# Reordering the hand-over from attention to the expert tiles in a fused two-layer kernel

## What is computed

```python
# layer 0, attention: summaries of 64-token chunks (4 sequences of 512), 16 heads, added to x
# layer 0, feed-forward block, _forward:
h = rmsnorm(x, ln1_w); q, k, v = ...            # 16 query heads, 4 key/value heads of 8
out = softmax(causal(q k^T / sqrt(8))) v         # over all 2048 tokens
out = out * sigmoid(out @ Wg + bg)
x = x + out @ Wo + bo
h2 = rmsnorm(x, ln2_w)
top1 = argmax(h2 @ Wr + br)                      # router, 8 experts
u = h2 @ W1[top1] + b1                           # up product, 128 -> 2 x 256
y = (u1 * sigmoid(u2)) @ W2[top1] + b2           # gate, down product
return x + y
# layer 1: a Mamba-like scan with 4 heads, then a ternary feed-forward part
```

## Time and profile before

| | us |
|---|---|
| median of 3 runs | 603.2 (603.0 to 603.21) |
| the profiled execution | 603.02 |
| its span | 600.9 |
| mean granted TensorE clock | 0.994 of full |
| busy: TensorE / ScalarE / VectorE / GpSimd | 562.0 / 470.0 / 399.1 / 120.8 |

### The profile page before, as it was taken

One profiled execution on the slowest core, in us unless ns is written; L12 is line 12 of the kernel. 1 busy time (PEld: TensorE's weight loads), 2 busy tenths in 40 slices (PEclk: granted clock), 3 DMA queues, 4 the chain that ended last, 5 costly groups with the idle time before them and its releaser, 6 DMA issues.

```text
span 600.9 us, 11244 instructions
## 1 busy us (share of the span) xinstructions
PE 562.0 (94%) x3944; PEld 330.8 (55%) x3944; DVE 399.1 (66%) x1060; ACT 470.0 (78%) x669; POOL 120.8 (20%) x161
## 2 busy tenths in 40 slices
PE   6899999999999999999887899698699999999998
PEld 3343434443443434333334587386478887887887
DVE  6784887666363453685527355887888788698773
ACT  5699999989899999999795366479598686685673
POOL 2063221120020030103601355112012010010010
PEclk9999999999999999999999999999999999999999
DMA  7212011024222210400317220200000000000000
GB/s 223 47 25 67 2 27 47 11 88 159 89 107 107 89 72 2 137 6 14 112 42 227 66 77 37 83 2 0 1 1 2 1 17 1 2 17 1 2 19 17
DMA packets 30982, 30.72 MB, mean 51 GB/s; under 512 B 6848, under 2 KB 20960, under 8 KB 30928
## 3 DMA queue, kind: packets, MB, share of 16 engines
q1 hardware_dynamic: 29680, 27.45, 14.6%
q0 software_dynamic: 1248, 2.57, 1.2%
HBM read 13.44 MB, written 12.89 MB: 44 GB/s over the span
## 4 chain that ended last, share of the span: by engine, by line
PE 70%; DVE 15%; ACT 7%; issue 6%; DMA 1%; POOL 0%; DVEq 0%; ACTq 0%; another core or an unknown queue 0%; POOLq 0%
PE ps L1414 18%; PE ps L1393 9%; PE ps L92 6%; PE ps L94 6%; PE ps L93 5%; ACT r L1002 3%; PE ps L1725 2%; PE ps L1494 2%; PE ps L1600 1%; PE ps L1307 1%; PE ps L1763 1%; PE ps L1766 1%; PE ps L1486 1%; PE ps L1730 1%; PE ps L1267 1%
## 5 line engine op out<-in xcount | busy, mean ns | idle before, releaser
L1002 ACT ACTIVATE r<-ps 128x1024 f32<-128x1024 f32 x272 | 257.5, 1041 | 19.6 <-PE ps L1393 17.0
L1414 PE MATMUL ps<-r 128*32 128x512 f32 (+3 forms) x1280 | 144.8, 539 | 0.9 <-DVE r L2185 0.5
L858 POOL TENSOR_SCALAR_AFFINE_SELECT r<-r 128x512 f32<-128x512 f32 (+1 forms) x80 | 47.0, 589 | 206.0 <-ACT r L1002 205.7
L1393 PE MATMUL ps<-r2r 32*128 32x512 f32 (+3 forms) x640 | 80.2, 445 | 4.2 <-ACT r L1002 2.5
L1393 PEld LDWEIGHTS ps<-r2r 32*128 32x128 f32 x640 | 35.6, 182 | 46.9 <-ACT r L1002 21.3
L901 POOL TENSOR_TENSOR r<-r 128x512 f32<-128x512 f32 x16 | 22.6, 1414 | 151.0 <-ACT r L1210 130.1
L1414 PEld LDWEIGHTS ps<-r 128*32 128x32 f32 x1280 | 27.7, 108 | 40.5 <-issue 27.3
L94 PE MATMUL ps<-r2r 128*128 128x512 f32 (+1 forms) x104 | 39.0, 375 | 0.0
L1279 PE MATMUL ps<-consts 128*128 128x512 bf16 x98 | 25.4, 400 | 8.4 <-DMA consts<-in_consts 4.4
L93 PE MATMUL ps<-r2r 128*128 128x512 f32 (+1 forms) x88 | 32.7, 372 | 0.0
L876 POOL DMA_INDIRECT rows_by_token<-r x23 | 23.6, 1025 | 23.8 <-ACT r L1065 14.1
(11 more groups left out here) (436 smaller groups left out, 1206.6 us busy)
## 6 DMA issues: line engine op xcount, KB each, us to landing
rows_by_expert<-r SPq DMA_DIRECT2D x34, 258.0 KB, 2.5
r2r<-r2r SPq DMA_DIRECT2D x56, 64.0 KB, 2.0
r<-in_f_W SPq DMA_DIRECT2D x1, 2048.0 KB, 9.4
r<-rows_by_expert SPq DMA_DIRECT2D x23, 64.5 KB, 1.8
res<-in_x SPq DMA_DIRECT2D x4, 256.0 KB, 4.0
r<-in_g_h1T SPq DMA_DIRECT2D x1, 1024.0 KB
r<-in_g_h2T SPq DMA_DIRECT2D x1, 1024.0 KB
r<-rows_by_token SPq DMA_DIRECT2D x4, 256.0 KB, 4.0
```

The source lines that it names most:

```text
L858: pool.affine_select(blk, blk, pattern, ALU.is_ge, nothing, base=0, channel_multiplier=-1).then_inc(s_msk, 1)
L1002: act.activation(probs[:, n % PBUFS, :, :], ps[:, b:b + 2, :], ACT.Exp).then_inc(s_exp, 1)
L1393: m = pe.matmul(ps[:, 2 * (n % SBUFS) + h, at:at + TB - query], kst[32 * j:32 * j + 32, group, P * kt:P * kt + P], qst[32 * j:32 * j + 32, ...
L1414: m = pe.matmul(ps[32 * j:32 * j + 32, 6, query:TB], vp[:, kt, group, :], probs[:, (2 * v + j // 2) % PBUFS, j % 2, at:at + TB - query], s ...
```

## The change

- **W1 high parts.** Eight pieces of 512 columns in place of four of 1024 (four after the last attention step, four behind `first_slots_copied`). VectorE's low piece n waits for high piece n. Low piece 6 moves from ahead of the read of LOGITS to the end of the early tiles, beside piece 7.
- **Router products first.** At the LOGITS step TensorE runs one `kept_busy` product in place of `first_up(1)`; `first_up(1)` now stands behind the router products.
- **Late rows.** The four `rows_scaled` instructions of VectorE go. ScalarE does them as Copy with a scale per partition: two after `up_tanh_of(1)`, two after `up_tanh_of(2)`. GpSimd's scatter of tile i waits for its own row tile.
- **Gate of the second early tile.** `activated(1)` stands between `late_expert` and `late_placed`, where VectorE would wait for the ranks, not behind them.
- **Row numbers ahead of experts.** VectorE computes `rows_of_tiles` before it copies `expert_i` and compares `pick`; the copy now has a settle of its own.
- **SyncE** reads two row numbers, not four, before it waits for the scatters.
- **Bias product.** In the loop the wait for the high rows stands behind the bias product, not ahead of it.

```diff
-        W1HIGH = [(w1f[:, a:a + 1024], w1h[:, a:a + 1024]) for a in range(0, 4096, 1024)]
-        W1LOW = [(w1f[:, a:a + 512], w1h[:, a:a + 512], w1l[:, a:a + 512]) for a in range(0, 4096, 512)]
+        W1SPLIT = [(w1f[:, a:a + 512], w1h[:, a:a + 512], w1l[:, a:a + 512]) for a in range(0, 4096, 512)]
@@ sync
-            ahead = [first_row(t) for t in range(AHEAD, AHEAD + 2 * GROUP)]
+            ahead = [first_row(t) for t in range(AHEAD, AHEAD + GROUP)]
             sp.wait_ge(s_scat, 16 * NT)
             for t in range(AHEAD, SLOTS):
-                r = ahead[t - AHEAD] if t < AHEAD + 2 * GROUP else first_row(t)
+                r = ahead[t - AHEAD] if t < AHEAD + GROUP else first_row(t)
@@ gpsimd
-                pool.wait_ge(s_h2, 2 if i < NT - 2 else 3)
+                pool.wait_ge(s_h2, 2 + i - (NT - TPB))
@@ scalar
+            def late_rows_scaled(tiles_of):
+                for i in tiles_of:
+                    act.activation(h2[i], xn[:, i, :], ACT.Copy, scale=hs2[:, i:i + 1]).then_inc(s_h2, 1)
@@
                 if k == STEPS:
-                    up_weights_high(0)
-                    up_weights_high(1)
+                    for n in range(0, 4):
+                        up_weights_high(n)
@@
             up_tanh_of(1)
+            act.wait_ge(s_mr, NAUX)
+            late_rows_scaled(range(NT - TPB, NT - 2))
             first_rows_copied(0)
             up_tanh_of(2)
+            late_rows_scaled(range(NT - 2, NT))
@@ tensor
                 elif k == LAST_CHAIN["LOGITS"]:
-                    first_up(1)
+                    kept_busy(1, 1)
@@
+            first_up(1)
             pe.wait_ge(s_moew2, 16)
             first_down(0)
             first_up(2)
@@
-                    pe.wait_ge(s_xsh, (t - AHEAD) // GROUP + 1)
                     pe.wait_ge(s_moea, t - 1)
                     pe.matmul(dst, pick[0:STACK, t:t + 1].broadcast_to([STACK, P]), biases[:, 0:2 * HID],
                               start=True, stop=False)
+                    pe.wait_ge(s_xsh, (t - AHEAD) // GROUP + 1)
@@ vector
-                    dve.wait_ge(s_whi, n // 2 + 1)
+                    dve.wait_ge(s_whi, n + 1)
@@
                 if (what, which) == ("LOGITS", NB - 1):
-                    up_weights_low(range(6, 7))
                     dve.wait_ge(s_sd2, 1)
@@
             late_expert()
-            rows_scaled(range(NT - TPB, NT - 2))
-            dve.sem_inc(s_h2, 1)
+            activated(1)
             late_placed()
-            rows_scaled(range(NT - 2, NT))
-            dve.sem_inc(s_h2, 1)
-            activated(1)
             dve.wait_ge(s_cnts, 2)
@@
-            step.mark(dve.tensor_copy(expert_i[:, at], expert[:, at]))
             step.alone(dve.tensor_reduce(lead_t[:, at], tiles_passed[:, at], X_AXIS, ALU.add))
-            dve.tensor_scalar(pick[:, at], expert[:, at], modulo, None, ALU.is_equal).then_inc(s_exp_t, 1)
             step.alone(dve.scalar_tensor_tensor(rows_f[:, at], tile_no[:, 0:n], early_used[:, 0:1], lead_t[:, at],
                                                 ALU.add, ALU.subtract))
             rows_of_tiles(at)
+            step.alone(dve.tensor_copy(expert_i[:, at], expert[:, at]))
+            dve.tensor_scalar(pick[:, at], expert[:, at], modulo, None, ALU.is_equal).then_inc(s_exp_t, 1)
@@
-            up_weights_low(range(7, 8))
+            up_weights_low(range(6, 8))
```

More of the change, by code:

```diff
@@ L965, in up_weights_high @@
                 act.wait_ge(s_pv, STEPS)
-                w, hi = W1HIGH[n]
+                w, hi, _ = W1SPLIT[n]
                 act.activation(hi, w, ACT.Copy).then_inc(s_whi, 1)
@@ L1017, in _ @@
                     first_slots_copied(1)
-                    up_weights_high(2)
-                    up_weights_high(3)
+                    for n in range(4, 8):
+                        up_weights_high(n)
                 if k in TANH_AT:
@@ L1571, in _ @@
             pe.wait_ge(s_exp_t, 2)
-            pe.wait_ge(s_wsp, len(W1LOW))
+            pe.wait_ge(s_wsp, len(W1SPLIT))
             for step_ in range(AHEAD, SLOTS + 2):
@@ L2074, in up_weights_low @@
                 for n in pieces:
-                    w, hi, lo = W1LOW[n]
+                    w, hi, lo = W1SPLIT[n]
                     if n == 4:
                         dve.wait_ge(s_biasd, 16)
-                    dve.wait_ge(s_whi, n // 2 + 1)
+                    dve.wait_ge(s_whi, n + 1)
                     dve.tensor_tensor(lo, w, hi, ALU.subtract).then_inc(s_wsp, 1)
```

## The result

The changed kernel took 605.63 us (median of 5, 604.75 to 606.84), the kernel before 603.2 (602.39 to 603.24). The ratio is 1.0047, with an interval of 1.003 to 1.0064. Forecast were 599.9 and "faster". The profiled execution is one of exactly 605.63, with a span of 603.6, so 2.7 us more than the 600.9 of before.

What follows compares the result with a forecast made beforehand. TensorE, finishing the five early tiles and then its fill, was taken to set the loop's start, 1.5 us behind the loads. Terms 1.1 + 2.0 + 0.35 - 0.2 = 3.25 gave a median of 599.9 us, range 599.2 to 601.6.

Steps and rivals of the forecast that it cites:

- the gate of tile 1: Early tiles: gate done at 325.0, so the transposes follow the rank sums at 326.7, not 327.76; 1.1 us gained.
- the sum: All terms up to the loop's start: 1.1 gate, 2.0 clock, 0.35 bias product, less 0.2 sixth load; 3.25 us.
- SyncE's first row load: Before the loop: issued at 334.2, 3.03 behind the last scatter's start at 331.1; hidden behind TensorE's fill.
- The multiplication rule: Late rows: Trainium skill sends multiplications to VectorE; set aside because ScalarE was idle there, cost 0, at most 0.2 us.
- the cover from 330.5 to the fill: Last early tiles: TensorE proceeds from tile 3's transposes without new waits, VectorE keeping pace, and starts the fill at 333.6.
- cover is thin there: VectorE's `activated(4)`: ready at 331.7, needed by TensorE at 331.8 or so; a miss costs its size.
- C: Early tiles: VectorE's `activated(4)`, ScalarE's queue or receipts take the gain back, leaving under 1.2 us; 602.5 us, chance 0.10.
- D: Loop: TensorE waits for row loads long enough that the clock falls to 1.2 GHz; slower, 606 us, chance 0.05.
- A: Start of the loop: row loads decide, landing 0.8 later than the fill's end; 600.7 us, chance 0.14.
- B: The clock falls all the same, say in the waits around 322; price 1.57 us, 601.5 us, chance 0.09.
- the fall of the clock: Early tiles, 328 to 332: without the idle ahead TensorE keeps 2.4 GHz; 2.0 us gained, 1.57 from the clock.
- the bias product's 0.35: Start of the loop: the bias product fits into the wait for the high rows; 0.35 us gained, once.

Runs made afterwards that it cites:

- g3: Changed kernel with 8 filling products ahead of the second product of tile 3 and 8 ahead of that of tile 4; 597.98 us, ratio 0.9965.
- f3: Changed kernel with the scaling of the late rows back on VectorE at its old places; 607.62 us, ratio 1.0065.
- h2: Changed kernel with the last six early scatters spaced and the early tiles' token scatters held until late row loads land; 596.19 us, ratio 0.9948.
- h1: Kernel before with its last six early scatters one per attention step; 599.54 us, ratio 1.0002.
- e8: Kernel before, unchanged, run once more for its profile; one run of 599.91 us.
- e7: Kernel before with 60 tiny GpSimd memsets right behind the twelve early scatters, from 299 to 310; 599.45 us, ratio 1.0006.
- e6: Kernel before with six fill products of TensorE ahead of the second early tile's transposes; 598.21 us, ratio 0.9981.
- f4: Kernel before with six filling products ahead of tile 1's transposes and the bias product ahead of the wait for late slots; 601.7 us, ratio 0.9973.
- e3: Changed kernel with GpSimd holding the five early token scatters until the loop's first rows are copied; 609.14 us, ratio 1.0102.
- e2: Changed kernel with the two 1 MB layer-1 weight loads issued behind the row loads of the expert tiles; 606.55 us, ratio 1.0045.
- e5: Changed kernel with every layer-1 weight load, small ones included, issued behind the row loads; 626.41 us, ratio 1.0449.
- g1: Changed kernel with every second-layer weight load behind the row loads, as in e5; one run of 627.1 us.
- f2: Kernel before with only the gate of tile 1 moved ahead of the first scaled late rows and late ranks on VectorE; 607.04 us, ratio 1.0053.
- e1: Changed kernel with the gate of the second early tile put back behind the destination rows; 607.49 us, ratio 1.0081.
- e4: Kernel before with 60 tiny GpSimd memsets, each waited for, from 312 on; 605.71 us, ratio 1.0037.
- g2: f4 with 60 single memsets on GpSimd from 312 on; 598.06 us, ratio 0.9973.
- f1: Changed kernel unchanged, run again beside the kernel before on chip 14; 606.77 us, ratio 1.0058.

## Why the prediction was wrong, point by point

**Bounds and the first steps: right in the main.** Up to 330.5 the changed trace follows the working. The rank sums were put at 326.7 and end at 326.9; the gate of tile 1 is off the path and L1344 follows them at once (forecast 326.7, measured 326.75 in the timeline); from the transposes of tile 1 to those of tile 3 the sum had 3.78, the traces have 330.49 - 326.75 = 3.74, and 3.76 in g3. The clock is 1.00 from 324 to 334. ScalarE's two pairs of late rows took 0.68 each and delayed nothing. SyncE's first row load was issued at 333.95, forecast 334.2, and here two errors cancel: the scatters began 0.56 later than before, not 0.3 (327.58, the last at 331.42), and the load came 2.53 behind the start of the last one, not 3.03. The multiplication rule that I set aside (the Trainium skill, "ScalarE: Activation LUTs", Rules for kernel authors) has f3 as its test: with the rows on VectorE, 607.62 against 606.77, no gain to be told, on a chip where both halt.

**The step that failed is the cover from 330.5 to the fill.** The prediction put the fill at 333.6, 3.1 us behind the transposes of tile 3. It began at 339.37. That stretch holds the hand-overs of tiles 3 and 4, in which ScalarE copies the transposes and TensorE waits for the copy. The sum took it over from the kernel before at its old length, without a term of its own; "cover is thin there" was said of VectorE's `activated(4)`, which came in time (331.57 for a forecast of 331.7). What gave way was ScalarE's start. The two idle times of TensorE, 3.55 and 2.39, took the place of some 0.47 each, as before had, which is 5.0 us; slow products took 0.29 + 1.03 for tile 4 in place of 0.56, which is 0.76. The fill then took 5.42 for 4.10, which is 1.32, at clocks of 0.50 and 0.52. Together 7.1, and the first product on rows is at 345.66 where 338.4 was forecast, 7.3 later. At that point the kernel is 345.66 - 342.26 = 3.4 behind before; 0.7 of it comes back later.

**The rivals.** C named ScalarE's queue, with the result "under 1.2 gained". It had no mechanism that could take more than the gain. D had the sign and half of the mechanism (TensorE waits, the clock falls to 1.2 GHz), but put it in the loop behind the row loads. The chance of "slower" was 0.05 because D demanded two or more falls of the clock of before's size; here two idle times and one low stretch behind them did it. A and B did not come: the row transposes wait for TensorE's fill alone; and the clock did not fall in the waits around 322. B is real at times all the same, and was priced too low. In the profiled runs of h2 and g3 the clock is 0.50 from 324 to 326, behind just those waits; they took 600.05 against a median of 596.19, and 601.98 against 597.98. That is 3.9 and 4.0 us in the slowest of 9 and of 11 runs, for a price of 1.57.

**The sum itself holds where nothing halts**, for the changed kernel with spaced scatters: 3.25 forecast, 3.5 (h2 against before) and 3.35 (h2 against h1) measured. That the medians agree so well is in part luck. The sum took the fall of the clock as certain in the kernel before, and it doesn't come in each execution: e8 has it, e7 has not. The runs of the kernel before show both. On the chips without halts those with a mean granted clock of 1.000 have medians of 598.04 (group 2, 5 runs), 598.15 (group 4, 3) and 597.92 (group 5, 6), those at 0.994 or less 599.39 (11), 600.32 (19) and 600.11 (12). So a fall, wherever in the run it lies, costs some 1.4 to 2.2 us, about the 1.57 to 2.0 of the sum, and e6's 1.0 is a median over runs with and without. Against the first sort of its own group h2 is 1.7 us ahead, against the second 3.9. f4 and e6 stand in different groups, 1.2 and 1.0 us below their before. They don't resolve the bias product's 0.35.

**What turns a gain of 3.3 us into a loss of 2.4 to 3.9** is that on chips of the first kind the moved work runs into halts, and the work of before in most of its executions does not, or only where nobody waits. (Of its 31 runs in group 3, 7 are slower than the changed kernel's fastest there, 605.23; why isn't shown.) What this costs is shown by the two kinds of chips: 0.9948 with spaced scatters on one, 1.0047 and 1.0058 on the others. h2 carries the spacing, so that part of the difference could be the spacing's on a halting chip; h1 says that it isn't on the other kind.

**What brings the halts is open.** Known: they go with the chip (or what surrounds it; chips 0 and 14 had them, 12 and 13 not, 13 at two times) and appear at two places, 293 to 302 and 331 to 341, plus the one that e3 made at 348. All lie in or just behind GpSimd's series of indirect scatters, and the series is the same on chips without halts. The halted instruction streams are ScalarE's, SyncE's and, in attention, VectorE's; TensorE stands still because it waits for ScalarE, and GpSimd's pauses of 0.63 and 2.25 in the changed kernel end 0.75 behind ScalarE's copy, as they do in the loop where nothing halts. The DMA engines are at 0.10 to 0.40 then, so it is no lack of bandwidth; the two 1 MB loads (e2) and the place of the row scaling (f3) are out. The other loads were moved (e5, g1) only where nothing halts. In the profile no packets of the instruction queues fall between 328 and 340, in the changed kernel or before, so that instruction fetch isn't seen to be the cause. f2 against f4 says that the 1.3 us of filling ahead of the early tiles' chain may decide whether the hand-overs are hit; the two differ also in a pause of GpSimd (1.18 against 0.30). That a pause in a series of scatters lets the others run is the guess that h1 and h2 were made for; no halting chip was had for it. A short pause is not enough: e1 and e4 have 0.81 and 0.94 in the same place and halt. And every run on record has the profiler's span and clock, so none shows whether the halts would come without its recording.

The Trainium skill has one mechanism that could join such streams: "NOTIFIC — the notification-queue block", 7.1, says that the block which writes out the event records of a core applies back-pressure inside rather than lose a record. No run here counts such records, and it wasn't tried.

## What to carry to other kernels

A hand-over that goes to and fro between two engines (here ScalarE copies, TensorE multiplies, for each tile) has no slack, and a late start of either end costs its full size, then again in TensorE's clock. Before moving such a chain to a new time, look in the trace of the old kernel for waits whose releaser had long been done or is "unknown", at any place, and see what other engines do there; where such waits exist, price the chain with one of them. And measure on more than one chip: the same change came out at 0.995 (with the scatters spaced) and at 1.005.

The kernel to keep is not the changed one: the kernel before with six filling products and the bias product ahead (f4) is faster on a chip with halts (0.9973), with six filling products alone on one without (0.9981), and so is f4 with 60 memsets that nobody needs (g2, 0.9973). If the chips were all of the second kind, it would be the changed kernel with spaced scatters (0.9948).

## What the runs showed of the hardware

- Two kinds of chips: 603.17 and 602.89 us (chips 0 and 14) against 599.21, 599.66 (chip 13, twice) and 600.1 (chip 12) for the same program, with a difference of 2.9 us in the spans of two profiles. ScalarE's waits of 1.02 and 2.36 us at 295 to 300 and VectorE's of 2.25 for 1.35 are in the slower one alone.
- Halts of 1 to 3 us of ScalarE with all inputs there. The longest idle time, 3.90 in f2, has 3.04 us of it: the product had ended at 335.62 and the copy starts at 338.66. Together with them go register moves of 655 ns instead of 29 on SyncE (697 in f2, 1289 in f3; f1 has none that long).
- An idle time of 1.42 us in the same place brought the clock to 0.58 in one profile of the kernel before and to 0.52 in another (e8), and left it at full in e4's and e7's. Idle times of 3.55 and 2.39 behind each other brought it to 0.50 in the changed kernel, and the fill was done at that level for the most part: 19 products of 128x512 in 5.42 us for 4.10.
